# A graph, attention and expert kernel: lists read in 24-byte pieces, later weight requests behind the third gather, another order in the tail

## The chip, the cores and the metric

The kernel runs on one core of a Trainium2 chip. The metric is device time in microseconds for one whole execution; lower is better. The profile comes from one separate, profiled execution.

## The reference, cut to what matters

1250 nodes of 1024 values go through a graph convolution and a linear attention in parallel, and then through a mixture of eight experts, of which each node uses two. The change touches only the experts:

```python
logits = flat @ Wr.T                          # flat: 1250 x 1024, Wr: 8 x 1024
weights, ids = jax.lax.top_k(logits, 2)
weights = softmax(weights)
h = einsum('nc,efc->nef', flat, W1)           # W1: 8 x 512 x 1024
val, gate = h[..., :256], h[..., 256:]
act = val * silu(gate)
expert_outputs = einsum('nef,ecf->nec', act, W2)   # W2: 8 x 1024 x 256
out = einsum('nec,ne->nc', expert_outputs, router_weights)
x = x + out
```

## The kernel before, in words

The layer norm, the graph convolution and the attention take the first four fifths of the time and aren't touched. They leave the residual in `out` and the normalised rows in `flat_d`, both in HBM. The router writes, for every expert, a list of entries (row number, weight; 8 bytes) into `list_d`, by scatters from GpSimd. A list has room for 13 tiles of 128 entries (`LT`), and entries that aren't taken point to filler rows behind row 1249, with weight 0.

The expert stage works on tiles of 128 entries. Each expert has `PER` = 3 tiles, so `TILES` = 24, three after three. Entries beyond 384 of an expert are done as further tiles ("items") in a loop at the end, whose length is read from a register and is at least 1; in the profiled execution it runs once. For a tile n:

- GpSimd gathers its rows from `flat_d` into `xg` (`gather`, six buffers, line 956), steered by `lists[:, n, 0]`.
- XE: TensorE turns the rows into `wide[0]` (line 2214), ScalarE copies them to the high part `xe_h`, VectorE subtracts to get the low part `xe_l`. Every product in this kernel is three products of such parts.
- GV: TensorE multiplies with the four slabs of W1 (line 2236) into `gv`, `kvb` for even and `lsb` for odd tiles, 24 matmuls.
- SM: ScalarE takes the silu of half of it into `sil`, VectorE multiplies it with the other half into `act`.
- TR: TensorE turns `act` (line 2220), ScalarE copies to `a_h`, VectorE subtracts to `a_l`.
- OUT: TensorE multiplies with W2 (line 2228, 12 matmuls), ScalarE scales into `y`, GpSimd scatters with addition into `out` (line 968).
- WP and W2P: each slab of W1 (512 KB, `ws_raw`, four buffers) and each W2 (1 MB, `w_raw`, one buffer) is loaded by SP and split by ScalarE (`ws_h`, `w_h`) and VectorE (`ws_l`, `w_l`). W2P covers one expert.

The order of ScalarE's and VectorE's work is written out in `expert_steps` (line 279); TensorE's is the loop over tiles below line 2240, which puts XE of tile n+1 and TR of tile n-1 inside GV of tile n, and OUT of tile n-1 behind it. The engines wait for each other by counters (`expert_full`, `expert_act`, `expert_dve`), whose values `numbered` works out from the same lists.

SP asks for the first expert's weights early, then, when the router is done, for the eight lists (line 829), one request each, 8-byte pieces, so that tile i of an expert holds entries 128 i to 128 i + 127. Right behind it asks for the next weights (line 705, 709), each as soon as its buffer is split. GpSimd starts the first six gathers as the lists land.

The tail begins behind GV of tile 23. Silu and product of tile 23 aren't in the ordinary steps; they and the further steps of the last tile are the head of the loop over items (`silu_tail`, `act_tail`, `finish`). One turn of that loop finishes the tile before (SM, TR, OUT), turns the item's rows, splits the item's weights, and runs the item's GV; on VectorE it then works out which item comes next (`item_link`, `next_item`, eight small operations on one partition, lines 1724 to 1730). Behind the loop the last item is finished in the same way. The list of the previous tile, which ScalarE's scale and the scatter need, is read again by SP once the scatter before has landed (lines 863, 875).

Of the kernel before, what the change touches and what calls it, by code (L numbers as in the profile page):

```python
# [16 lines left out]
F32 = mybir.dt.float32  # L17
# [6 lines left out]
ALU = mybir.AluOpType  # L24
ACT = mybir.ActivationFunctionType
# [253 lines left out]
def expert_steps():  # L279

    o = [("WP", m) for m in range(SLABS_PER)] + [("W2P", 0), ("XE", 0)]
    for n in range(TILES):
        e, i = divmod(n, PER)
        if e + 1 < EXP:
            o += ([("W2P", e + 1)] if i == PER - 1 else
                  [("WP", SLABS_PER * (e + 1) + 2 * i), ("WP", SLABS_PER * (e + 1) + 2 * i + 1)])
        if n >= 2:
            o.append(("OUT", n - 2))
        if n + 1 < TILES:
            o.append(("XE", n + 1))  # L290
        if n >= 1:
            o.append(("TR", n - 1))
        o.append(("GV", n))
        if n < TILES - 1:
            o.append(("SM", n))
    return o + [("OUT", TILES - 2)]


# [4 lines left out]
for _n in range(TILES):  # L303
    ORDERED_PE += [("XE", _n + 1)] if _n + 1 < TILES else []
    ORDERED_PE += ([("TR", _n - 1)] if _n else []) + [("GV", _n)] + ([("OUT", _n - 1)] if _n else [])
R_FULL = numbered({"XE", "TR", "GV", "OUT"}, [("XE", 0)] + [k for k in ORDERED_PE if k != ("GV", TILES - 1)])
SCATTERED = [len(range(s, TILES - 1, NY)) for s in range(NY)]


def build(nc, x, src_cols, dst_cols, dst_groups, slabs, wv, w1, w2, wr, proj, feat_rows, consts, turns, tie,  # L310
          iota, keys, eye, pe, blank, before, list_blank, tokens, expert_at, item_rows, b2_rows, out):
    ctx = ExitStack()
    with ctx:
# [327 lines left out]
        def _(sp):  # L641
# [183 lines left out]
            sp.wait_ge(routed, 1)  # L825
            sp.wait_ge(lists_free, 1)
            list_tiles = list_d.rearrange("(t q) w -> t q w", q=RT_)
            for e in range(EXP):
                sp.dma_start(lists[:, PER * e:PER * e + PER, :],
                             list_tiles[LT * e:LT * e + PER].rearrange("i q w -> q i w")).then_inc(list_landed[min(e, 2)], 16)  # L830
            for k in STEPS:
                if k[0] == "WP" and k[1] + SLABS_PER < SLABS_PER * EXP:
                    sp.wait_ge(expert_dve, R_DVE[k])
# [166 lines left out]
        def _(act):  # L1000
# [237 lines left out]
                    else:  # L1238
                        ins.then_inc(expert_act, 1)

            def silu_tail(turn, tr_full):

                act.wait_ge(tail_gv, turn)
                act.wait_ge(expert_dve, R_DVE[("SM", TILES - 2)])
                act.activation(sil[:, :], gv[1][:, 0:FF], ACT.Silu).then_inc(tail_act, 1)
                act.wait_ge(tail_full, tr_full)
                copy(a_p[1][0][:, :, :].rearrange("p f c -> p (f c)"), turned[1]).then_inc(tail_act, 1)

# [7 lines left out]
            act.wait_ge(items_ready, 1)  # L1256
            items = act.value_load(items_n[0:1, 0:1], min_val=1, max_val=MAX_ITEMS)
            with act.Fori(0, items) as r:
                silu_tail(r + 1, r * 3 + 2)
                copy(xe_p[0][0][:, :, :], blocks(wide[0], KD, RT_, 128)).then_inc(tail_act, 1)  # L1260
                for m in range(SLABS_PER):
                    if m == 2:
                        out_tail(r * 3 + 3, r * 16 + 16, r * 16 + 16 * SCATTERED[NY - 1])
                    act.wait_ge(ws_landed[m], r * 16 + 16 * (EXP + 1))
                    copy(ws_p[m][0][:, :, :], ws_raw[m][:, :, :]).then_inc(tail_act, 1)
                act.wait_ge(w2_landed, r * 16 + 16 * (EXP + 1))
                copy(w2_p[1][0][:, :, :], w2_raw[:, :, :]).then_inc(tail_act, 1)
            silu_tail(items + 1, items * 3 + 1)
            out_tail(items * 3 + 2, items * 16 + 16, items * 16 + 16 * SCATTERED[NY - 1])


        @block.vector
        def _(dve):
# [472 lines left out]
            for k in STEPS:  # L1746
                kind, n = k
                if kind == "WP":
                    hi, lo = ws_p[n % (2 * SLABS_PER)]
                    acted(k)  # L1750
                    ins = tt(lo[:, :, :], ws_raw[n % SLABS_PER][:, :, :], hi[:, :, :].bitcast(F32), ALU.subtract)
                    if n >= SLABS_PER * (EXP - 1):
                        ins.then_inc(raw_split, 1)
                        dve.wait_ge(raw_split, n - SLABS_PER * (EXP - 1) + 1)
                        dve.sem_inc(expert_dve, 1)
                    else:
                        ins.then_inc(expert_dve, 1)
                elif kind == "W2P":
                    hi, lo = w2_p[n % 2]
                    acted(k)  # L1760
                    ins = tt(lo[:, :, :], w2_raw[:, :, :], hi[:, :, :].bitcast(F32), ALU.subtract)
                    if n == EXP - 1:
                        ins.then_inc(w2_split, 1)
                        dve.wait_ge(w2_split, 1)
                        dve.sem_inc(expert_dve, 1)
                    else:
                        ins.then_inc(expert_dve, 1)
                elif kind == "XE":
                    hi, lo = xe_p[n % 2]
                    acted(k)  # L1770
                    ins = tt(lo[:, :, :], blocks(wide[0], KD, RT_, 128), hi[:, :, :].bitcast(F32), ALU.subtract)
                    if n == TILES - 1:
                        ins.then_inc(tail_xe, 1)
                        dve.wait_ge(tail_xe, 1)
                        dve.sem_inc(expert_dve, 1)
                    else:
                        ins.then_inc(expert_dve, 1)
                elif kind == "SM":
                    acted(k)
                    if n >= 2:  # L1780
                        dve.wait_ge(expert_full, R_FULL[("TR", n - 2)])
                    tt(act_t[n % 2][:, :], gv[n % 2][:, FF:2 * FF], sil[:, :], ALU.mult).then_inc(expert_dve, 1)
                elif kind == "TR":
                    hi, lo = a_p[n % 2]
                    acted(k)
                    tt(lo[:, :, :].rearrange("p f c -> p (f c)"), turned[n % 2],
                       hi[:, :, :].bitcast(F32).rearrange("p f c -> p (f c)"), ALU.subtract).then_inc(expert_dve, 1)

            def act_tail(turn):

                dve.wait_ge(tail_act, turn * 8 + 1)
                tt(act_t[1][:, :], gv[1][:, FF:2 * FF], sil[:, :], ALU.mult).then_inc(tail_low, 1)
                dve.wait_ge(tail_act, turn * 8 + 2)
                tt(a_p[1][1][:, :, :].rearrange("p f c -> p (f c)"), turned[1],
                   a_p[1][0][:, :, :].bitcast(F32).rearrange("p f c -> p (f c)"), ALU.subtract).then_inc(tail_low, 1)

            items = dve.value_load(items_n[0:1, 0:1], min_val=1, max_val=MAX_ITEMS)
            with dve.Fori(0, items) as r:
                act_tail(r)
                dve.wait_ge(tail_act, r * 8 + 3)  # L1800
                tt(xe_p[0][1][:, :, :], blocks(wide[0], KD, RT_, 128), xe_p[0][0][:, :, :].bitcast(F32), ALU.subtract
                   ).then_inc(tail_xe, 1)
                for m in range(SLABS_PER):
                    dve.wait_ge(tail_act, r * 8 + m + 4)
                    tt(ws_p[m][1][:, :, :], ws_raw[m][:, :, :], ws_p[m][0][:, :, :].bitcast(F32), ALU.subtract
                       ).then_inc(raw_split, 1)
                dve.wait_ge(tail_act, r * 8 + 8)
                tt(w2_p[1][1][:, :, :], w2_raw[:, :, :], w2_p[1][0][:, :, :].bitcast(F32), ALU.subtract
                   ).then_inc(w2_split, 1)
                dve.wait_ge(item_read, r + 1)  # L1810
                item_link(ts(item_x[:, 2:3], first, GAP, ALU.add), r)
                next_item(r)
                dve.sem_inc(item_made, 1)
            act_tail(items)


        @block.tensor
        def _(ten):
# [429 lines left out]
            for n in range(TILES):  # L2248
                e = n // PER
                dved(("XE", n))  # L2250
                for kt in range(KD):
                    m = SLABS_PER * e + kt // 2
                    if n % PER == 0 and kt % 2 == 0:
                        dved(("WP", m))
                    mm = gate_value_part(n % 2, xe_p[n % 2], ws_p[m % (2 * SLABS_PER)], kt)
                    if kt == 1 and n + 1 < TILES:
                        expert_rows(n + 1)
                    if kt == 3 and n:
                        dved(("SM", n - 1))
                        act_turned((n - 1) % 2).then_inc(expert_full, 1)  # L2260
                mm.then_inc(expert_full if n < TILES - 1 else tail_gv, 1)
                if n:
                    dved(("TR", n - 1))
                    dved(("W2P", (n - 1) // PER))
                    if n >= 2:
                        ten.wait_ge(expert_act, R_ACT[("OUT", n - 2)])
                    out_product((n - 1) % 2, w2_p[(n - 1) // PER % 2]).then_inc(expert_full, 1)
# [103 lines left out]
```

## Time and profile before

| | |
|---|---|
| median of 3 timed runs | 1466.77 us (1465.06 to 1468.51) |
| the profiled execution's own time | 1471.01 us |
| its span, first to last instruction | 1469.3 us |
| TensorE matmul busy in the span | 1382.0 us (94%) |
| mean granted clock of TensorE | 0.977 |
| VectorE, ScalarE, GpSimd busy | 60%, 36%, 11% |
| DMA queue 1 (requests of SP) | 33.5% of the 16 engines' span |
| DMA queue 0 (requests of GpSimd) | 16.0% |

Busy shares are means over stages with different limits. In the page's 40 slices TensorE is busy nine tenths or more nearly throughout; slice 33, from about 1175 to 1212 us, shows 2 tenths, and the last shows 4.

### The profile page before, as it was taken

Reading aid. Unit: us, or ns where it says so; the run is one execution under the profiler, and the core shown is the slowest. Engines: PE = TensorE matmul, PEld = TensorE weight load, DVE = VectorE, ACT = ScalarE, POOL = GpSimd, SP = SyncE. Lnnn points to the kernel's source line nnn. Section 1 sums busy time; section 2 is a strip of 40 time slices with the busy share of each in tenths; the row PEclk is TensorE's granted clock in tenths of the full one; section 3 lists DMA queues with packets and bytes.
Section 4 is the critical chain, followed back from the end, with each engine's and each line's share of the span. In section 5 each row is a group of like instructions: output and inputs, shape, how many; then the busy total and the mean of one; then the engine's idle time right before and its main releaser. Section 6 shows DMA issues by size and latency. Waiting matters only on the chain.

```text
span 1469.3 us, 19184 instructions
## 1 busy us (share of the span) xinstructions
PE 1382.0 (94%) x7433; PEld 1266.9 (86%) x7433; DVE 875.9 (60%) x1600; ACT 534.3 (36%) x629; POOL 166.7 (11%) x169
## 2 busy tenths in 40 slices
PE   6999999999999999899999999999999929999994
PEld 5788989999999999899999999999878728888883
DVE  6455668788787787636656333355567854444423
ACT  4223245454444544423122133322211235555523
POOL 0011211101101101000000000000000531222211
PEclk9999999999999999999999999999999959999997
DMA  9865422432432434867453033221564577888843
GB/s 299 245 156 125 88 52 32 99 81 31 98 78 35 98 78 101 309 152 195 107 146 104 15 99 110 67 85 35 144 184 140 140 242 219 226 227 230 230 101 57
DMA packets 99181, 193.22 MB, mean 132 GB/s; under 512 B 33905, under 2 KB 64617, under 8 KB 97372
## 3 DMA queue, kind: packets, MB, share of 16 engines
q1 hardware_dynamic: 79171, 145.83, 33.5%
q0 software_dynamic: 19920, 46.17, 16.0%
q8 instruction: 59, 0.97, 0.3%
q14 instruction: 31, 0.25, 0.1%
HBM read 129.38 MB, written 72.21 MB: 137 GB/s over the span
## 4 chain that ended last, share of the span: by engine, by line
PE 74%; DMA 11%; DVE 8%; ACT 4%; issue 2%; POOLq 0%; SPq 0%; ACTq 0%; POOL 0%; DVEq 0%
PE slot L2032 23%; PE slot L2119 13%; DMA adj_d<-stage 6%; PE slot L2189 5%; PE slot L2228 5%; PE kvb L2236 5%; PE lsb L2236 4%; PE slot L1988 3%; PE kvb L2153 3%; PE slot L2001 3%; PE slot L1974 2%; PE slot L1963 2%; PE slot L2214 2%; DMA mix_d<-mixn 1%; PE slot L1943 1%
## 5 line engine op out<-in xcount | busy, mean ns | idle before, releaser
L2032 PE MATMUL slot<-big_hi,slab_h 128*128 128x418 f32 x768 | 194.6, 362 | 10.1 <-DVE qp_l L1558 4.8
L2032 PE MATMUL slot<-big_lo,slab_h 128*128 128x418 f32 x768 | 189.3, 355 | 0.0
L2032 PE MATMUL slot<-big_hi,slab_l 128*128 128x418 f32 x768 | 188.4, 354 | 0.0
L2032 PEld LDWEIGHTS slot<-big_hi,slab_h 128*128 128x128 f32 x768 | 139.7, 190 | 15.0 <-DVE qp_l L1558 6.4
L2032 PEld LDWEIGHTS slot<-big_hi,slab_l 128*128 128x128 f32 x768 | 145.3, 189 | 2.2
L2032 PEld LDWEIGHTS slot<-big_lo,slab_h 128*128 128x128 f32 x768 | 145.3, 189 | 2.0
L908 POOL DMA_DIRECT2D adj_d<-stage x80 | 67.3, 842 | 485.0 <-ACT stage L1012 328.5
L2119 PE MATMUL slot<-adj,xs_h 125*128 125x418 f32 x480 | 118.1, 354 | 0.5 <-DVE ztmp L1283 0.5
L2119 PE MATMUL slot<-adj,xs_l 125*128 125x418 f32 x480 | 117.5, 353 | 0.0
L1287 DVE TENSOR_SCALAR oh_src<-lane,src_lo 125x125 bf16<-125x125 f16 x320 | 83.7, 262 | 30.0 <-PE kvb L1848 21.0
L2119 PEld LDWEIGHTS slot<-adj,xs_h 125*128 125x128 f32 x480 | 90.5, 189 | 1.7 <-DVE ztmp L1283 0.7
L2119 PEld LDWEIGHTS slot<-adj,xs_l 125*128 125x128 f32 x480 | 90.5, 189 | 1.2
L1287 DVE TENSOR_SCALAR oh_key<-key_iota,key_rel 125x240 bf16<-125x240 int16 x320 | 90.2, 282 | 0.0
L933 POOL DMA_INDIRECT list_d<-rec,spots x20 | 28.1, 1404 | 521.8 <-issue 504.5
L1283 DVE TENSOR_TENSOR slab_l<-slab_raw,slab_h 128x1024 fp32r<-128x1024 f32 x34 | 41.6, 1223 | 48.7 <-ACT slab_h L1012 48.5
L1572 DVE RECIPROCAL nrm<-nrm 128x1254 f32<-128x1254 f32 x8 | 63.9, 7993 | 9.6 <-ACT nrm L1012 9.6
L1283 DVE TENSOR_TENSOR xe_l<-slot,xe_h 128x1024 fp32r<-128x1024 f32 x25 | 30.6, 1224 | 62.2 <-ACT xe_h L1012 62.2
L1541 DVE SCALAR_TENSOR_TENSOR kk_l<-slot,kk_h 125x512 fp32r<-125x512 f32 x80 | 52.2, 687 | 23.6 <-ACT kk_h L1146 22.8
L1146 ACT ACTIVATE kk_h<-slot 125x512 fp32r<-125x512 f32 x80 | 47.5, 596 | 44.7 <-PE slot L1963 44.3
L1558 DVE SCALAR_TENSOR_TENSOR qp_l<-slot,qp_h 128x1254 fp32r<-128x1254 f32 x30 | 43.9, 1464 | 29.6 <-ACT qp_h L1158 29.6
L968 POOL DMA_INDIRECT out_dram<-y,lists x23 | 36.3, 1578 | 169.4 <-ACT y L1012 142.3
L2153 PE MATMUL kvb<-kk_h,v_h 125*128 125x256 f32 x160 | 47.1, 295 | 6.7 <-DVE kk_l L1541 6.7
(334 smaller groups left out, 2902.4 us busy)
## 6 DMA issues: line engine op xcount, KB each, us to landing
slab_raw<-slabs_dram SPq DMA_DIRECT2D x40, 512.0 KB, 4.3
ws_raw<-w_dram SPq DMA_DIRECT2D x36, 512.0 KB, 4.8
adj_d<-stage POOLq DMA_DIRECT2D x81, 117.2 KB, 3.1
w_raw<-w_dram SPq DMA_DIRECT2D x9, 1024.0 KB, 5.4
adj_d<-eye_dram POOLq DMA_DIRECT2D x1, 6250.0 KB, 24.0
raw<-adj_d SPq DMA_DIRECT2D x3, 1828.8 KB
dx<-x_dram SPq DMA_DIRECT2D x10, 448.0 KB
xn_d<-dx SPq DMA_DIRECT2D x10, 448.0 KB
```

Of the source, the lines that this page charges most:

```text
L908: pool.dma_start(adj_d[:, bass.ds(first, SPAN), :].rearrange("p d j -> p (d j)"), stage[g % 3][:, :], accum_op=ALU.add).then_inc(e_added, 16)
L1146: act.activation(kk_p[k[2] % 3][0][:, :], kk_bank(k), ACT.Relu).then_inc(act_done, 1)
L1283: return dve.tensor_tensor(o, a, b, op)
L1287: dve.tensor_scalar(o, a, s1, None, op0)
L1541: dve.scalar_tensor_tensor(out=kk_p[k[2] % 3][1][:, :], in0=kk_bank(k), scalar=0.0, in1=kk_p[k[2] % 3][0][:, :].bitcast(F32), op0=ALU.max, ...
L1572: link(dve.reciprocal(nrm[:, :], nrm[:, :]))
L2032: mm = ten.matmul(ps[:, 512 * q:512 * q + CW], w[a][:, kt, :], big[b][:, kt, CW * q:CW * q + CW], start=(kt == 0 and c == 0), stop=(kt == ...
L2119: mm = ten.matmul(ps[:, 512 * q:512 * q + CW], xs_p[t % 2][a][:, j, :], adj[:, j, CW * q:CW * q + CW], start=(j == 0 and a == 0), stop=(j ...
L2153: mm = ten.matmul(kvb[:, FEAT * h:FEAT * h + FEAT], v_p[a][:, i, 64 * h:64 * h + 128], kk_p[i % 3][b][:, FEAT * h:FEAT * h + FEAT], start= ...
L2189: mm = ten.matmul(ps[:T, 512 * q:512 * q + 512], big[b][:, kt, T * i:T * i + T], rows_p[kt][a][:, 512 * q:512 * q + 512], start=(kt == 0 a ...
L2228: mm = ten.matmul(wide[1][:RT_, 512 * q:512 * q + 512], a_p[s_][a][:, f, :], w_[b][:, f, 512 * q:512 * q + 512], start=(f == 0 and c == 0) ...
L2236: mm = ten.matmul(gv[s_][:RT_, :], xe[a][:, kt, :], w_[b][:, kt % 2, :], start=(kt == 0 and c == 0), stop=(kt == KD - 1 and c == 2))
```

## The change

It does three things.

1. SP reads the lists of the first seven experts with partition q taking the three neighbouring entries 3q to 3q+2 of the list, one piece of 24 bytes, so tile i of these experts holds the entries 3q + i. The last expert's list is read tile by tile as before.
2. Between the lists and the later weight requests SP waits until the gathers 0, 1 and 2 have landed.
3. The silu and product of tile 23 go into the ordinary steps. The item loop begins with the transposed copy (`high_tail`, `low_tail`) and ends with silu and product of the item; VectorE works out the next item at the head of the loop; ScalarE makes three slab copies ahead of the previous tile's output instead of two.

```diff
@@ expert_steps
-        o.append(("GV", n))
-        if n < TILES - 1:
-            o.append(("SM", n))
+        o += [("GV", n), ("SM", n)]
@@ SP
-            for e in range(EXP):
-                sp.dma_start(lists[:, PER * e:PER * e + PER, :],
-                             list_tiles[LT * e:LT * e + PER].rearrange("i q w -> q i w")).then_inc(list_landed[min(e, 2)], 16)
+            for e in range(EXP - 1):
+                sp.dma_start(lists[:, PER * e:PER * e + PER, :].rearrange("q i w -> q (i w)"),
+                             list_d[LIST * e:LIST * e + CAP, :].rearrange("(q i) w -> q (i w)", i=PER)
+                             ).then_inc(list_landed[min(e, 2)], 16)
+            sp.dma_start(lists[:, TILES - PER:TILES, :], list_tiles[LT * (EXP - 1):LT * (EXP - 1) + PER].rearrange("i q w -> q i w")
+                         ).then_inc(list_landed[2], 16)
+            for n in range(3):
+                sp.wait_ge(gathered[n], 16)
             for k in STEPS:
@@ ScalarE
-            def silu_tail(turn, tr_full):
-
-                act.wait_ge(tail_gv, turn)
-                act.wait_ge(expert_dve, R_DVE[("SM", TILES - 2)])
-                act.activation(sil[:, :], gv[1][:, 0:FF], ACT.Silu).then_inc(tail_act, 1)
+            def high_tail(tr_full):
+
                 act.wait_ge(tail_full, tr_full)
                 copy(a_p[1][0][:, :, :].rearrange("p f c -> p (f c)"), turned[1]).then_inc(tail_act, 1)
@@
             with act.Fori(0, items) as r:
-                silu_tail(r + 1, r * 3 + 2)
+                high_tail(r * 3 + 2)
                 copy(xe_p[0][0][:, :, :], blocks(wide[0], KD, RT_, 128)).then_inc(tail_act, 1)
                 for m in range(SLABS_PER):
-                    if m == 2:
+                    if m == 3:
                         out_tail(r * 3 + 3, r * 16 + 16, r * 16 + 16 * SCATTERED[NY - 1])
@@
                 copy(w2_p[1][0][:, :, :], w2_raw[:, :, :]).then_inc(tail_act, 1)
-            silu_tail(items + 1, items * 3 + 1)
+                act.wait_ge(tail_gv, r + 1)
+                act.activation(sil[:, :], gv[1][:, 0:FF], ACT.Silu).then_inc(tail_act, 1)
+            high_tail(items * 3 + 1)
@@ VectorE
-            def act_tail(turn):
+            def low_tail(turn):
 
                 dve.wait_ge(tail_act, turn * 8 + 1)
-                tt(act_t[1][:, :], gv[1][:, FF:2 * FF], sil[:, :], ALU.mult).then_inc(tail_low, 1)
-                dve.wait_ge(tail_act, turn * 8 + 2)
                 tt(a_p[1][1][:, :, :].rearrange("p f c -> p (f c)"), turned[1],
@@
             with dve.Fori(0, items) as r:
-                act_tail(r)
+                dve.wait_ge(item_read, r + 1)
+                item_link(ts(item_x[:, 2:3], first, GAP, ALU.add), r)
+                next_item(r)
+                dve.sem_inc(item_made, 1)
+                low_tail(r)
...
                 tt(w2_p[1][1][:, :, :], w2_raw[:, :, :], w2_p[1][0][:, :, :].bitcast(F32), ALU.subtract
                    ).then_inc(w2_split, 1)
-                dve.wait_ge(item_read, r + 1)
-                item_link(ts(item_x[:, 2:3], first, GAP, ALU.add), r)
-                next_item(r)
-                dve.sem_inc(item_made, 1)
-            act_tail(items)
+                dve.wait_ge(tail_act, r * 8 + 8)
+                tt(act_t[1][:, :], gv[1][:, FF:2 * FF], sil[:, :], ALU.mult).then_inc(tail_low, 1)
+            low_tail(items)
```

## Rows read from the trace of the kernel before

**Rows 1.** Busy time by stretch: us, each engine (instructions), clock, DMA share, GB/s

```profile
1260.00:1430.00 170.00, 170.00 (x837) 141.63 (x836) 71.14 (x80) 79.77 (x97) 44.29 (x35) 1.00 0.78 205
```

**Rows 2.** The chain that ended last, 1190 to 1220: start us, us, what

```profile
1197.49 8.44 DMA xg<-flat_d,lists
1206.07 1.96 PE slot L2214 x8
...
1219.11 1.36 PE lsb L2236 x6
```

**Rows 3.** Order of time, 1190 to 1216: start, us, engine, line, out<-in, count [idle before]

```profile
1194.58 4.12 SPq L829 DMA_DIRECT2D lists<-list_d  x8
1196.45 2.29 DVE L1283 TENSOR_TENSOR w_l<-w_raw,w_h 128x2048 fp32r<-128x2048 f32 x1
1197.49 2.12 POOL L956 DMA_INDIRECT xg<-flat_d,lists  x1 [5.64 <-DMA lists<-list_d]
1198.74 2.00 SPq L705 DMA_DIRECT2D ws_raw<-w_dram  x4
1199.91 0.96 POOL L956 DMA_INDIRECT xg<-flat_d,lists  x1 [0.30 <-issue]
...
1215.04 1.03 ACT L1012 ACTIVATE xe_h<-slot 128x1024 fp32r<-128x1024 f32 x1 [4.08 <-PE slot L2214]
```

**Rows 4.** DMA view: packets 1202 to 1203; time to landing of the gather of 1453.79

```profile
q1 hardware_dynamic: 58, 0.22, 53.0%
q0 software_dynamic: 42, 0.17, 50.2%
...
xg<-flat_d,lists POOLq DMA_INDIRECT x1, 3.9
```

**Rows 5.** Order of time, VectorE and GpSimd about 1162, GpSimd at 1454

```profile
1161.61 1.22 DVE L1615 SCALAR_TENSOR_TENSOR acc<-acc,xm 125x1024 f32<-125x1024 f32 x1
1161.69 2.21 POOL L933 DMA_INDIRECT list_d<-rec,spots  x1 [0.30 <-issue]
...
1453.79 1.00 POOL L990 DMA_INDIRECT xg<-flat_d,lists  x1 [8.90 <-DMA lists<-list_d]
```

**Rows 6.** DMA view, landing: second slab of 1199.3, gathers 1194.5 to 1215, scatter 1443.3

```profile
ws_raw<-w_dram SPq DMA_DIRECT2D x1, 512.0 KB, 7.0
...
xg<-flat_d,lists POOLq DMA_INDIRECT x6, 11.0
...
out_dram<-y,lists POOLq DMA_INDIRECT x1, 6.0
```

**Rows 7.** The chain that ended last, 1429 to 1458

```profile
1429.58 2.74 PE slot L2228 x12
...
1434.36 0.39 ACT sil L1245
...
1435.73 0.39 ACT a_h L1012
...
1436.62 4.63 PE slot L2228 x12
...
1452.85 5.03 PE slot L2228 x12
```

**Rows 8.** Busy time by stretch, the output product of tile 23

```profile
1436.60:1440.20 3.60, 3.58 (x9) 2.81 (x10) 3.14 (x3) 2.31 (x3) 0.00 (x0) 0.53 0.74 127
```

**Rows 9.** Order of time, ScalarE and VectorE from 1436.9 to 1451

```profile
1436.91 2.00 ACT L1012 ACTIVATE ws_h<-ws_raw 128x1024 fp32r<-128x1024 f32 x2
...
1441.42 1.12 ACT L1012 ACTIVATE y<-slot,lists 128x1024 f32<-128x1024 f32 x1 [2.51 <-PE slot L2228]
...
1444.33 1.91 ACT L1012 ACTIVATE w_h<-w_raw 128x2048 fp32r<-128x2048 f32 x1
...
1446.27 2.29 DVE L1283 TENSOR_TENSOR w_l<-w_raw,w_h 128x2048 fp32r<-128x2048 f32 x1 [0.39 <-ACT w_h L1012]
...
1448.48 0.13 DVE L1287 TENSOR_SCALAR item_x<-item_w 1x1 int32<-1x1 f32 x1
...
1450.57 0.42 DVE L1283 TENSOR_TENSOR act<-lsb,sil 128x256 f32<-128x256 f32 x1 [0.41 <-DVE item_w L1730]
```

More of the change, by code:

```diff
@@ L305 @@
     ORDERED_PE += ([("TR", _n - 1)] if _n else []) + [("GV", _n)] + ([("OUT", _n - 1)] if _n else [])
-R_FULL = numbered({"XE", "TR", "GV", "OUT"}, [("XE", 0)] + [k for k in ORDERED_PE if k != ("GV", TILES - 1)])
+R_FULL = numbered({"XE", "TR", "GV", "OUT"}, [("XE", 0)] + ORDERED_PE)
 SCATTERED = [len(range(s, TILES - 1, NY)) for s in range(NY)]
@@ L1781, in _ @@
                         dve.wait_ge(expert_full, R_FULL[("TR", n - 2)])
-                    tt(act_t[n % 2][:, :], gv[n % 2][:, FF:2 * FF], sil[:, :], ALU.mult).then_inc(expert_dve, 1)
+                    tt(act_t[n % 2][:, :], gv[n % 2][:, FF:2 * FF], sil[:, :], ALU.mult
+                       ).then_inc(expert_dve if n < TILES - 1 else tail_low, 1)
                 elif kind == "TR":
@@ L1798, in _ @@
             with dve.Fori(0, items) as r:
-                act_tail(r)
[L1800 to L1809, printed above, removed]
                 dve.wait_ge(item_read, r + 1)
@@ L1813, in _ @@
                 dve.sem_inc(item_made, 1)
-            act_tail(items)
+                low_tail(r)
+                dve.wait_ge(tail_act, r * 8 + 2)
+                tt(xe_p[0][1][:, :, :], blocks(wide[0], KD, RT_, 128), xe_p[0][0][:, :, :].bitcast(F32), ALU.subtract
+                   ).then_inc(tail_xe, 1)
+                for m in range(SLABS_PER):
+                    dve.wait_ge(tail_act, r * 8 + m + 3)
+                    tt(ws_p[m][1][:, :, :], ws_raw[m][:, :, :], ws_p[m][0][:, :, :].bitcast(F32), ALU.subtract
+                       ).then_inc(raw_split, 1)
+                dve.wait_ge(tail_act, r * 8 + 7)
+                tt(w2_p[1][1][:, :, :], w2_raw[:, :, :], w2_p[1][0][:, :, :].bitcast(F32), ALU.subtract
+                   ).then_inc(w2_split, 1)
+                dve.wait_ge(tail_act, r * 8 + 8)
+                tt(act_t[1][:, :], gv[1][:, FF:2 * FF], sil[:, :], ALU.mult).then_inc(tail_low, 1)
+            low_tail(items)
         @block.tensor
@@ L2260, in _ @@
                         act_turned((n - 1) % 2).then_inc(expert_full, 1)
-                mm.then_inc(expert_full if n < TILES - 1 else tail_gv, 1)
+                mm.then_inc(expert_full, 1)
                 if n:
```

## The prediction

> **What bounds the kernel now.** I read the busy times by stretch first, then the chain of work that ended last, then the order of time and the DMA views around the two places the change touches. The stretch table shows that from 1260 to 1430 us TensorE is busy 170.00 of 170 us at the full clock while the 16 DMA engines are 0.78 busy [rows 1]. Nothing in the change takes work from TensorE there, so the middle of the expert stage can't move. What can move is the stall ahead of it and the tail behind it. In the chain the stall reads: the first gather is issued at 1197.49 and lands 8.44 us later, TensorE turns its rows at 1206.07 (1.96 us), and after their split it has product after product; tile 1's begins at 1219.11 [rows 2]. In the tail TensorE, ScalarE and VectorE take turns on the chain.
>
> **Start: what the moved weight requests are worth.** Before, SP asks for slabs 4 to 7 and the second W2 from 1198.74 on, right behind the lists, and so before the first gather has moved a byte [rows 3]. In the microsecond from 1202 both kinds run together: 58 packets of q1 (weights), 42 of q0 (gather), each at about half of the engines' time [rows 4]. The gather of the same 128 rows that runs with no other large traffic, the one issued at 1453.79, lands in 3.9 us [rows 4]. Its issuing instruction takes 1.00 us against 2.12 for the first gather [rows 3, 5], so I add 1.1 and get 5.0: landing at 1197.49 + 5.0 = 1202.5 in place of 1205.9. **Gain 3.4 us**, if everything behind it follows; the low clock of TensorE's first products moves along, since it starts from the same idle state. Both ends: 0 if the weights aren't what delays it; 8.44 - 3.9 = 4.5 at most, if the long issue goes too.
>
> **Start: what the 24-byte lists are worth.** Seven lists of 128 pieces replace seven of 384. SP spends 4.12 us on eight requests [rows 3]; that may fall by a microsecond, and the first list may land some 0.2 to 0.3 us sooner. I cost this at nothing, because the first gather's instruction seems to be held by something else. VectorE is in w_l, with two SBUF inputs, from 1196.45 to 1198.74; 2.12 us after 1197.49 is 1199.61, and that is 1198.74 plus 0.87, about the 0.96 that the next gather takes [rows 3]. The same picture stands at 1161.69: a scatter that starts inside a VectorE operation (until 1162.83) takes 2.21 us and ends 1.07 behind it [rows 5]. So a gather that starts 0.3 us sooner still ends its issue at 1199.6. The Trainium skill says the same of the mechanism (SBUF — State Buffer, "SBUF: two separate sides"): VectorE and GpSimd share a port pair as an exclusive lock, held for a whole instruction. By that rule the sooner list is worth 0; without it the gather would land at 1197.2 + 3.9 = 1201.1, 1.4 us sooner still. The other six lists were never waited for. The interleaved order puts as many rows of 4 KB into each gather and scatter as before, some of them filler rows in each tile rather than nearly all in the third: cost 0, with the cover that the DMA engines have 22% free.
>
> **Start: what the added wait costs.** Behind SP's wait for gather 2 stand the weights of expert 1. GpSimd starts a gather every 1.25 us, so gather 2 lands about 1201.2 + 3.9 = 1205.1, up to 1206. The second slab request landed 7.0 us after its issue while sharing with gathers [rows 6]. Hence slab 4 lands by about 1210 and slab 5 between 1211.2 (the bytes of all gathers and two slabs at the 400 GB/s seen there) and 1205.7 + 7.0 = 1212.7. ScalarE takes slabs 4 and 5 in order *ahead* of the second tile's rows (xe_h), where it stood idle 4.08 us before [rows 3]. With everything 3.4 us earlier, tile 1's product can start at 1219.11 - 3.4 = 1215.7 [rows 2]; slab 5 at 1212.7 gives split 1213.7, xe_h 1214.8, xe_l by 1216.2: a stall of 0.5 us at worst, none at 1211.2. Slabs 6 and 7 and W2 are split one and two tiles later and have some microseconds. I take 0.
>
> **Tail, first half.** Today the last tile's silu waits until the item loop has begun: sil at 1434.36, product with the gate, transposes, a_h at 1435.73 [rows 7]. After the change silu and product of tile 23 run in the ordinary order at 1429.6, while TensorE still does the 2.74 us output product of tile 22, and the transposes follow the row transposes at 1433.2. ScalarE's loop entry stays, so a_h comes at 1434.36: **1.37 us** sooner, and tile 23's output product starts at 1435.25 and not 1436.62. It took 4.63 us on the chain, 4.46 to the next product's first matmul, because the clock had fallen (granted 0.53 of full, so 1.2 GHz for nearly all of it [rows 8]) after TensorE had done next to nothing since 1433.2. Now it has stood only 1.8 us, so I expect full clock and 2.74: 1.7 us more. ScalarE then goes three ws_h (1.0 us each, from 1435.54), y (1.12), ws_h, w_h (1.91): done at 1442.5; VectorE's w_l (2.29) ends at 1444.8 against 1448.56 today [rows 9]: **3.8 us** sooner. If the clock falls all the same, y comes at 1439.8 and this is 2.5.
>
> **Tail, second half.** Today eight small VectorE operations on the item list stand between w_l and the last product with the gate: from 1448.48 to 1450.57 [rows 9]. They move to the loop's start, where VectorE has only to be done by a_h at 1434.75; they take 1.7 us from about 1431, so they are covered by ScalarE's y and loop entry (uncovered they would cost up to 1.7). That takes **2.0 us** more off, so the last act starts at 1444.8 and not 1450.57, 5.8 us sooner. From act to the last output product today takes 2.28 us at low clock, and from sil's act to tile 23's product 1.85 [rows 7, 9]; I take 1.85: start at 1446.65. The product itself takes 5.0 at low clock today; I take 4.55, as the clock still falls in this gap half the time. It ends at 1451.2. The last y also needs the last list, which SP asks for once tile 23's scatter has landed: issue about 1440.5 (0.8 behind y, which ends at 1439.7), 6.0 us as today [rows 6] to 7.8 with the gather now right behind it, list 1.8 more: between 1448.3 and 1450.1, just in time. So y starts at 1451.3 in place of 1458.06: **6.8 us** for the tail. Ends: 4.5 (clock low twice) and 7.9 (clock full twice, then the list is late).
>
> **Sum.** The profiled execution took 1471.01 us, with a span of 1469.3; 3.4 + 6.8 = 10.2 leaves 1460.8 and 1459.1. The median of the timed runs is 1466.77, 4.2 below the profiled one, and the stages are the same, so I subtract from it: **1456.6 us**.
>
> **Rivals.** (1) The first gather doesn't land sooner: its 8.44 us would then be list packets and first use, not weights. Against it stands that q0 got half of each microsecond from 1202; for it, that the list packets of 8 bytes share the engines just before. Only the tail is gained: 1466.8 - 6.8 = 1460.0. (2) Clock low in tile 23's output product: 1.3 us less, 1457.9. (3) Late weights: slab 5 later than 1212.2 costs one for one. If gather 2 took 11.0, the median of today's first six [rows 6],, slab 5 would land at 1219.7 and stall 7 us: 1463.9. (4) Slower than before: DMA becomes the bound. If rows scattered over the whole node range, and filler rows in every tile, made gathers and scatters dearer, the 0.78 share [rows 1] would reach 1 at 28% more; from there each per cent costs 0.0726 us in each of 22 tiles, 1.6 us. It decides from 34% on, where the 10 us are used up; at 40% the time is 1456.6 + 19 = 1476. Nothing in the trace speaks for it: both orders read rows of 4 KB. (5) The change doesn't do what it says the other way: the issue isn't held by VectorE, and the sooner list counts: 1.4 us more, 1455.2.
>
> **Numbers.** Forecast 0.60 (own range 1454 to 1459), gather unmoved 0.13, clock low 0.12, late weights 0.07, DMA bound 0.02, sooner list 0.06. The range 1453 to 1461.5 covers all but most of the late weights and the DMA bound, and leaves 1.5 us for how medians of one kernel differ (1465.06 to 1468.51 before). About 0.2%, 2.9 us, is what a measurement can tell, so faster means under 1463.8: 0.93; within 0.04; slower 0.03.
>
> **What would show it.** The first gather's time to landing: near 5 us. TensorE's first transposes about 8.1 us behind the first list request's issue, where they are 11.5 behind it now. No idle TensorE ahead of tile 1's product. The issue of the first gather still about 2.1 us long. In the tail the last act's idle time ended by w_l or silu, not by item_w; tile 23's output product at full clock. The forecast is wrong if the first gather still takes over 7 us, if TensorE stands before tile 1's product, or if the last list lands behind the last output product by microseconds.

## The result, and the profile after

The median is 1459.48 us of six runs (1457.73 to 1462.0), beside 1468.99 of six of the kernel before: ratio 0.9941, interval [0.9925, 0.9957]. The profiled execution took 1460.71 us with a span of 1459.0, against 1471.01 and 1469.3, so 10.3 us less where the prediction's sum had 10.2. Both halves have the predicted sign, and both were mis-sized: y of tile 22 starts at 1430.06 and not 1432.34, so all ahead of it gave 2.28 us and not 3.4 (0.33 of it, 1194.58 to 1194.25, was there at SP's first list request, where nothing had changed yet); from there to the last y it is 17.64 us and not 25.72, so the tail gave 8.08 and not 6.8. That the two errors nearly cancel in this profile is luck; how much the tail's share of it varies is shown below.

The chain of work that ended last, changed kernel (start us, us, what), at the start of the expert stage:

```profile
1194.25 2.23 DMA lists<-list_d
...
1197.43 4.82 DMA xg<-flat_d,lists
...
1202.38 1.96 PE slot L2217 x8
...
1206.52 6.51 DMA ws_raw<-w_dram
...
1213.05 1.07 ACT ws_h L1015
...
1216.56 1.65 PE lsb L2239 x6
```

The gather takes 4.82 where [rows 2] has 8.44. But in [rows 2] the chain goes from the gather through the turning and the split of tile 0's rows, and from there on TensorE alone to tile 1's product; now it leaves TensorE behind that split and passes through a weight slab that SP asked for at 1206.52. That is a new wait, and the order of time shows what it costs (start, us, engine, line, out<-in, count [idle before]):

```profile
1197.43 1.47 POOL L959 DMA_INDIRECT xg<-flat_d,lists  x1 [6.29 <-DMA lists<-list_d]
1206.14 1.83 SPq L703 DMA_DIRECT2D ws_raw<-w_dram  x4
1211.76 1.06 ACT L1015 ACTIVATE ws_h<-ws_raw 128x1024 fp32r<-128x1024 f32 x1 [6.37 <-DMA ws_raw<-w_dram]
1213.05 1.06 ACT L1015 ACTIVATE ws_h<-ws_raw 128x1024 fp32r<-128x1024 f32 x1 [0.23 <-DMA ws_raw<-w_dram]
1216.56 0.50 PE L2239 MATMUL lsb<-ws_h,xe_h 128*128 128x512 f32 x1 [1.50 <-DVE xe_l L1285]
```

ScalarE waits for slab 4, then for slab 5, and tile 1's xe_h stands behind them; TensorE idles 1.50 us. Counted from the first list request, tile 1's product begins at 22.31 where it was 24.36. (The chain of [rows 2] writes 1219.11 for it, the end of the matmul before; its own first matmul started at 1218.94, in the order of time:)

```profile
1218.94 0.39 PE L2236 MATMUL lsb<-ws_h,xe_h 128*128 128x512 f32 x1
```

The DMA view says why the slabs are late; packets and MB of queues 0 (gathers) and 1 (weights), from 1208 to 1209 and from 1209 to 1210:

```profile
q0 software_dynamic: 86, 0.32, 80.9%
q1 hardware_dynamic: 7, 0.03, 9.1%
...
q1 hardware_dynamic: 67, 0.27, 72.6%
q0 software_dynamic: 28, 0.07, 17.5%
```

The weights were asked for at 1206.14, and 2.9 us later they had moved 7 packets: gathers 3 to 5 were in the queues first. Not all of the 2.9 is owed to them. In the trace the first weight packet comes 2.3 us behind the request; in the kernel before, with no packet of a gather ahead of it, it came 1.1 behind (at 1199.86, for the request at 1198.74).

The middle of the stage, busy time by stretch as in [rows 1]: TensorE is as full as before, with the DMA engines at 0.80. (The 0.78 of [rows 1] is over ten microseconds more; from 1260 to 1420 the kernel before has 0.79.) From the transposes of tile 2 to y of tile 22 both kernels take 212.0 us.

```profile
1260.00:1420.00 160.00, 160.00 (x791) 133.37 (x791) 69.43 (x77) 77.89 (x94) 41.40 (x32) 1.00 0.80 209
```

The tail. First both output products by stretch (clock is the third number from the end), then the chain:

```profile
1432.93:1435.80 2.87, 2.87 (x13) 2.19 (x13) 2.43 (x3) 2.87 (x4) 0.65 (x1) 1.00 0.63 66
1444.28:1447.20 2.92, 2.92 (x12) 2.14 (x12) 0.00 (x0) 0.00 (x0) 0.00 (x0) 1.00 0.64 208
```

```profile
1430.06 1.12 ACT y L1015
...
1432.02 6.21 DMA out_dram<-y,lists
...
1439.28 6.35 DMA out_dram<-y,lists
...
1445.85 1.74 DMA lists<-list_d
...
1447.70 1.12 ACT y L1015
```

The two products took 4.63 and 5.03 in [rows 7]; the first of them had a clock of 0.53 in its first 3.6 us [rows 8], and the second, from 1452.85 to its end, one of 0.57. Now both run at full clock (2.4 GHz), and neither is on the chain: it runs over scatter 22, for which GpSimd waits, scatter 23, the last list, and the last y, for which ScalarE idles 4.12 us until the list is there. The last output product ends at 1447.26, the list lands 0.3 us later and y begins at 1447.70, so TensorE and the DMA chain are nearly level.

### The profile page after: what moved, and what is told of

Read it like the earlier page. It is cut to its first block, busy times and chain, and to the rows that moved or that the text cites. A ratio compares the mean times of both kernels' runs of the same rounds, so it can differ in the third digit from the quotient of the medians.

```text
span 1459.0 us, 19184 instructions
## 1 busy us (share of the span) xinstructions
PE 1377.8 (94%) x7433; PEld 1264.4 (87%) x7433; DVE 876.8 (60%) x1600; ACT 534.7 (37%) x629; POOL 167.1 (11%) x169
## 4 chain that ended last, share of the span: by engine, by line
PE 74%; DMA 12%; DVE 7%; ACT 3%; issue 2%; POOLq 0%; SPq 0%; POOL 0%; ACTq 0%; DVEq 0%
PE slot L2035 24%; PE slot L2122 13%; DMA adj_d<-stage 6%; PE slot L2192 5%; PE lsb L2239 5%; PE slot L2231 4%; PE kvb L2239 4%; PE slot L1991 3%; PE slot L2004 3%; PE kvb L2156 3%; PE slot L1977 2%; PE slot L1966 2%; PE slot L2217 1%; DMA mix_d<-mixn 1%; PE slot L1946 1%
## 5 line engine op out<-in xcount | busy, mean ns | idle before, releaser
L1289 DVE TENSOR_SCALAR oh_src<-lane,src_lo 125x125 bf16<-125x125 f16 x320 | 84.0, 263 | 29.1 <-PE kvb L1851 20.4
L1161 ACT ACTIVATE qp_h<-slot 128x1254 fp32r<-128x1254 f32 x30 | 36.6, 1219 | 45.8 <-PE slot L1977 45.1
```

The costliest lines, as they stand in the source:

```text
L1289: dve.tensor_scalar(o, a, s1, None, op0)
```

## The experiments

Three times are compared below: from SP's first list request to the row transposes of tile 2 ("start", 25.73 before, 23.80 after), from there to y of tile 22 (212.0 wherever TensorE's clock is full by then), and from there to the last y ("tail", 25.72 and 17.64). What lies ahead of the first list request varies between executions by more than most effects here (that request is issued between 1187.65 and 1198.56); a single time says little, the stage times much more. They vary too: the changed kernel's start, run in four profiles with nothing altered in it (after, items_late, busy_tail, after_again), took 23.80, 24.41, 24.63 and 24.25, and the start before 25.73 and 25.79 (tail_only). Most experiments below have one profile, so a start between 23.8 and 24.6 is no news.

Five kernels were timed once each: rows_first 1466.21, w2_behind_rows 1466.24, items_late 1463.44 and busy_tail 1456.97, beside one execution of the kernel before of 1467.52, and busy_start 1457.59 beside one of 1463.90. Nothing is concluded from these times.

**The wait alone.** The kernel before with

```diff
+            for n in range(3):
+                sp.wait_ge(gathered[n], 16)
             for k in STEPS:
```

> The kernel before with only the added wait of SP for gathers 0, 1 and 2. Theory (weights delay the first gather): the first gather, still issued about 2.1 us long, lands 5 us after its issue instead of 8.4; slab 5 comes about 1.5 us too late for tile 1, as in the changed kernel; tile 1's product starts 2.0 us sooner than before, so the time is about 0.15% less. Rival (list packets or first use delay it): the first gather still takes over 7 us, and the late weights make the time longer by about 1.5 us.

Ratio 1.0 [0.9982, 1.0018]. In its profile the rows of tile 0 are turned 5.66 us behind the gather's issue (8.58 before), tile 1's product waits 1.75 us for the late slabs and begins 1.5 sooner (22.85 behind the first list request, not 24.36), where 2.0 had been expected; the start is 24.37. That is 1.4 gained, too little for the times to show, and within what the changed kernel's start takes with the new lists.

**The lists alone.** The kernel before with the diff's two new list requests.

> The kernel before with only the seven lists in pieces of 24 bytes. Theory: SP's eight list requests take 3.6 us instead of 4.1, the weights are asked for half a microsecond sooner, the first gather's issue still ends 0.9 us behind VectorE's w_l, and it lands no sooner than before (8.0 to 9.0 us); the DMA share from 1260 to 1430 stays 0.78; time within 0.1% of before. Rival (list packets were in the gather's way): it lands in 5 to 6 us and 2 us come off. Rival (scattered rows are dearer): the DMA share goes up by 0.05 or more.

Ratio 0.9998 [0.9977, 1.0019]. SP is done with the lists 0.5 us sooner (weights asked for 3.69 behind the first list request, not 4.16). The rows of tile 0 are turned 9.36 behind the gather's issue, and the start is 26.73, 1.0 worse in this one profile. Some 0.4 of that is not owed to the lists: w_l, and with it the issue, ended later behind the first list request (5.45, not 5.03). The other 0.5 lies behind the issue's end (6.96 for 6.46), and goes with weights that are asked for sooner. The chain that ended last, lists alone:

```profile
1197.33 9.22 DMA xg<-flat_d,lists
...
1206.69 1.95 PE slot L2217 x8
```

Its order of time shows VectorE's hold again: the gather starts inside w_l, takes 2.40, and ends 0.9 behind it, after the first weight request:

```profile
1196.56 2.28 DVE L1286 TENSOR_TENSOR w_l<-w_raw,w_h 128x2048 fp32r<-128x2048 f32 x1
1197.33 2.40 POOL L959 DMA_INDIRECT xg<-flat_d,lists  x1 [5.36 <-DMA lists<-list_d]
1197.97 1.91 SPq L705 DMA_DIRECT2D ws_raw<-w_dram  x4
```

The DMA share is 0.80 from 1260 to 1420, against 0.79 before, and TensorE is busy throughout: the interleaved order costs nothing there.

**The tail alone.** The kernel before with the third part of the diff.

> The kernel before with only the change of the tail (silu of tile 23 in the ordinary steps, next item at the head of the loop, three slab copies ahead of y). Theory: from the end of tile 22's output product to the last y 17.6 us instead of 25.7, 8 us less, nothing changed ahead of it: ratio about 0.9945. Rival (the tail's gain hangs on the moved start through the clock's phase): 5 to 6.5 us less, with TensorE at half clock in one of the two last output products.

1460.8 us, ratio 0.9957 [0.9941, 0.9974]: most of what the whole change brings. Its tail is 18.84, 6.9 less than before, between the 8 of the theory and the 5 to 6.5 of the rival: the clock fell in tile 23's product (0.66 from 1432 to 1437) and was full in the last.

**Waiting for one gather and not three.** The changed kernel with

```diff
-            for n in range(3):
-                sp.wait_ge(gathered[n], 16)
+            sp.wait_ge(gathered[0], 16)
```

> The changed kernel, but SP waits for gather 0 alone before it asks for slabs 4 to 7. Theory (the wait for the third gather costs a stall of 1.5 us of TensorE ahead of tile 1's product): requests at 1202.3, slab 5 landed by about 1210, no idle TensorE before tile 1, gather 0 still about 4.8 us; 1.5 us less than the changed kernel. Rival (slabs are late because gathers hold the engines whatever the request's time): slab 5 lands no sooner than 1212 and the stall stays. Rival: gather 1 becomes late and tile 0's product stops for it.

1457.71 us, 0.9924 [0.99, 0.9948], overlapping the changed kernel's interval. The weights are asked for 3.3 us sooner, but ScalarE still waits for both slabs:

```profile
1211.22 1.06 ACT L1014 ACTIVATE ws_h<-ws_raw 128x1024 fp32r<-128x1024 f32 x1 [4.14 <-DMA ws_raw<-w_dram]
1213.78 1.06 ACT L1014 ACTIVATE ws_h<-ws_raw 128x1024 fp32r<-128x1024 f32 x1 [1.50 <-DMA ws_raw<-w_dram]
```

The stall ahead of tile 1's product falls from 1.50 to 0.43, the start to 23.44, 0.4 below the lowest of the four. Slab 5 came far later than expected: for two microseconds from the request at 1203.96 all packets are gathers'. When the weights are asked for matters less than what is queued ahead of them.

**Rows ahead of slabs.** The changed kernel with XE of tile 1 ahead of slabs 4 and 5 on ScalarE and VectorE.

```diff
     for n in range(TILES):
+        if n == 0:
+            o.append(("XE", 1))
...
-        if n + 1 < TILES:
+        if n and n + 1 < TILES:
```

> The changed kernel, with tile 1's rows (xe) ahead of slabs 4 and 5 in the written order of ScalarE and VectorE. Theory (ScalarE waits for the late slabs 4 and 5 while tile 1's rows lie ready): the slabs land as late as in the changed kernel, 6.9 us or more after the rows' request order begins, but TensorE doesn't stop ahead of tile 1's product (idle under 0.2 us in place of 1.5), and from the first list request to tile 2's row transposes 22.3 us instead of 23.8. Rival (slabs late for their own use): the stop only moves, to slab 8's product or to tile 2, and no time comes off.

TensorE has no idle time ahead of tile 1's product, but the start is 23.65 and not the 22.3 expected. Part of it is the gather: tile 0's rows came at 8.72 behind the first list request (8.13 in the changed kernel, 8.13 to 9.15 in the four profiles). From there to tile 2's row transposes it is 14.93 us, against 15.48 to 15.79 in the four, so taking the stall away is worth 0.6 to 0.9. The rest went to the clock: tile 0's product was at half clock until 10.0 us behind the turning of its rows, 8.3 in the changed kernel.

**The issue freed, with no wait.** The kernel before with one swap in ScalarE's and VectorE's order, so that the split of the first W2 (w_h on ScalarE, w_l on VectorE) comes behind tile 0's rows:

```diff
-    o = [("WP", m) for m in range(SLABS_PER)] + [("W2P", 0), ("XE", 0)]
+    o = [("WP", m) for m in range(SLABS_PER)] + [("XE", 0), ("W2P", 0)]
```

> The kernel before, with the split of the first W2 (w_h, w_l) moved behind the rows of tile 0 on ScalarE and VectorE, so that VectorE is idle when the first gather is issued. Theory (the issue is held by w_l): the first gather's issuing instruction takes 0.9 to 1.2 us instead of 2.1. Rival (a first gather is slow by itself): 2.1 us as before. It still shares the engines with the weights, so it lands 7.5 us or more after its issue.

```profile
1195.50 1.00 POOL L956 DMA_INDIRECT xg<-flat_d,lists  x1 [6.80 <-DMA lists<-list_d]
1196.22 2.15 SPq L705 DMA_DIRECT2D ws_raw<-w_dram  x4
...
1195.50 5.57 DMA xg<-flat_d,lists
...
1214.30 1.36 PE lsb L2236 x6
```

(order of time, then the chain that ended last). The issue takes 1.00 and not 2.12, as expected. The gather then lands in 5.57 though the weights are asked for as early as before, where I had expected 7.5 or more. There is no stall, and the start is 23.43: 2.3 us gained, no less than the changed kernel gains, and SP waits for nothing. So weights asked for early don't by themselves make the gather as late as it was. The runs without SP's wait line up by the order of the two: the end of the first gather's issue is measured against SP's first weight request; then, behind the issue's end, the gather's first packet of 4 KB in the trace, and the turning of the rows.

| kernel | issue ends behind the weight request | first packet behind the issue's end | rows turned behind the issue's end |
|---|---|---|---|
| best (below) | 0.18 | 0.75 | 4.69 |
| w2_behind_rows | 0.28 | 0.72 | 4.70 |
| hold_free (below) | 0.54 | 2.01 | 4.84 |
| before | 0.87 | 2.10 | 6.46 |
| tail_only | 1.02 | 2.88 | 6.60 |
| lists_only | 1.76 | 3.32 | 6.96 |
| eight with the wait | (weights much later) | 0.69 to 0.72 | 3.45 to 3.84 |

With nothing ahead of it the gather's first packet comes 0.7 behind the issue's end, and the first weight packet 1.1 behind its request (1.11 to 1.13 in hold_free, before, tail_only and lists_only). In best and w2_behind_rows the gather's packets are first, and the weights' first comes 2.7 and 2.5 behind the request; in the other four the weights are first and the gather starts late. That order doesn't explain everything. In hold_free the weights were first too, and the rows were in time all the same; and with the gather first it still takes 0.8 to 1.3 us more than with the weights held back. How late a gather lands once it has begun stays open.

**The item's operations back at the end.** The changed kernel with VectorE's item steps again between w_l and the last act.

> The changed kernel, but the eight small VectorE operations on the item list stand again between w_l and the last product with the gate. Theory: the last act starts 2.0 us behind w_l's end instead of at once, all else equal; TensorE then idles 3.3 us ahead of the last output product and is at half clock in it, so from the end of tile 22's output product to the last y 21 to 23 us, against 17.6 in the changed kernel's profile. Rival (the last list or the scatter sets the end): last y within 1 us of the changed kernel's, as they start at the same time.

The tail is 20.80, 3.2 more. TensorE stands 3.10 us ahead of the last transposes (1.19 in the changed kernel), so 1.9 is the operations themselves; the rest is the clock, 0.64 in the last product, which takes 4.48 and not 2.98. Expected were 21 to 23, so the effect is there at a little under the lower end; and as the low clock came in four of the seven tails below too, only the 1.9 is surely owed to the operations.

**TensorE kept busy in the tail.** The changed kernel with 5, 4 and 3 products that nobody reads, in the waits around the two output products:

```diff
                 act_turned(1).then_inc(tail_full, 1)
+                keep_busy(5 if turn is not items else 3, 0)
...
                 mm.then_inc(tail_gv, 1)
+            keep_busy(4, 0)
```

> The changed kernel with 5, 4 and 3 products that nobody reads, put on TensorE where it waits in the tail: ahead of tile 23's output product, ahead of the last transposes, ahead of the last output product. Theory (the tail's length hangs on whether the clock falls in these waits: 17.6 us without a fall, 18.8 with one, 20.4 with two): clock 1.00 from 1431 to the last output product, 17.4 to 17.9 us from tile 22's output product to the last y. Rival (the clock falls by its own time): a granted clock of 0.5 in one of the two output products all the same.

The clock stays full and the tail is 17.57, level with the changed kernel's profile: there the clock had held by itself. That is not the rule. Of seven tails with this order and no extra products, the last output product ran at full clock in three and at 0.62 to 0.64 in four (wait_for_one, rows_first, busy_start, hold_free), and tile 23's product was slow in two (wait_for_one, tail_only). With no fall the tail is 17.6 to 17.9, with one 18.8 to 19.0, with two 20.4. TensorE's idle times ahead of the products are the same in all seven (1.8, then 1.2 to 1.3 and 1.1 us), so nothing that I can see in the trace decides it. With the extra products both were at full clock in two tails of two (busy_tail and best), without them in two of seven (after, after_again): that points their way, but two profiles don't prove it.

**TensorE kept busy at the start.** The changed kernel with 18 such products between the first weights' split and the first rows, and 6 between the rows and tile 0's product:

```diff
+            dved(("WP", 3))
+            early(18)
             expert_rows(0)
+            early(6)
```

> The changed kernel with 18 more products of 128 x 512 between the split of the first expert's weights and the first rows, and 6 between the turning of those rows and the first tile's product; nobody reads what they write. They stand in time in which TensorE waits for the lists and the first gather. If the low clock of the first tile's product is owed to TensorE having stood idle before it, the granted clock is full from the first tile on, and with it tile 0's product takes some 1.5 to 2 us less; but then the stall before tile 1's product (1.50 in the changed kernel) grows by as much, since the late slabs set when tile 1 can start: from the first list request to tile 2's row transposes still 23.0 to 23.8 us. If instead TensorE's own work sets that time, it falls by 1.5 to 2 us to about 22. The rival that the clock doesn't depend on it gives the same clock as in the changed kernel. Tail as in the changed kernel, 17.6, or 18.8 if the clock falls once.

```profile
1196.28 1.08 PE L2217 MATMUL slot<-ident,xg 128*128 128x128 f32 x8
1197.12 1.64 PE L2253 MATMUL lsb<-ws_h 128*128 128x512 f32 x6
1199.73 0.50 PE L2239 MATMUL kvb<-ws_h,xe_h 128*128 128x512 f32 x1 [0.97 <-DVE xe_l L1285]
...
1210.37 0.50 PE L2239 MATMUL lsb<-ws_h,xe_h 128*128 128x512 f32 x1 [3.98 <-DVE xe_l L1285]
```

The rows are turned in 1.08 and not 1.94 us, and tile 0's product at full clock ends before 1206.4; the stall grows from 1.50 to 3.98 and the start is 24.35, no better. The clock falls again in the longer stall (0.50 from 1212 to 1214), and this costs beyond the start: from there to y of tile 22 it is 213.5 us in place of 212.0. With the wait in SP, the late slabs set when tile 1 begins, and what TensorE saves ahead of them is lost, here with 1.5 us more.

**Without the wait, and the best of it.** On the same chip: the changed kernel again; "hold_free", the changed kernel without SP's wait and with the swap of the W2 split; "best", which is hold_free with the unread products at the start and in the tail.

> The changed kernel once more, for a direct comparison with the two kernels that follow: 1459.5 us, 8 below the kernel before.

> The changed kernel without SP's wait for gathers 0 to 2, and with the split of the first W2 behind the split of tile 0's rows. If the gather came late because VectorE held its issue until the weights were ahead of it in the queues, freeing the issue does what the wait does: the first gather's issue takes 1.0, its rows are turned 5.7 behind it, no stall ahead of tile 1's product, from the first list request to tile 2's transposes 23.4 (changed kernel 23.8), the median within 1 us of the changed kernel. If the wait is what keeps the weights out of the gather's way (asked for 3.7 behind the first list request with the new lists, and not 4.2), the first gather takes 8 or more again and the time is 2 to 3 us above the changed kernel.

> hold_free with the products that nobody reads, both at the start (18 and 6) and in the tail (5, 4, 3). With the weights asked for early nothing late stands behind tile 0's product, so here the full clock should count, where with the wait it didn't: tile 0's rows turned in 1.1 and not 1.9, its product 6.5 and not 8.1; tile 1's product 19.1 to 20 behind the first list request, no stall, tile 2's transposes at 20.7 to 21.5, against 23.8 in the changed kernel. The tail stays 17.6. Median 2 to 3.5 us below the changed kernel: 1456 to 1457.5. If the slabs, which then share the engines with six gathers, come later than tile 0's product ends, most of it turns into a stall and the median is that of the changed kernel.

| kernel | median us | ratio to before | start | tail |
|---|---|---|---|---|
| after_again | 1460.97 | 0.9946 [0.9927, 0.9965] | 24.25 | 17.90 |
| hold_free | 1459.72 | 0.9939 [0.9907, 0.9970] | 24.02 | 18.82 |
| best | 1454.88 | 0.9908 [0.9887, 0.9928] | 19.83 | 17.52 |

hold_free takes away the wait with no loss that shows (the intervals overlap): the issue takes 1.00, the rows are turned 5.84 behind it, no stall. In best, from the split of the first rows on, the chain is TensorE alone:

```profile
1198.95 1.24 DVE xe_l L1283
1200.23 1.65 PE kvb L2237 x6
1201.89 0.87 PE slot L2215 x8
1202.76 4.13 PE kvb L2237 x18
1206.89 1.36 PE lsb L2237 x6
```

The start is 19.83, somewhat under the 20.7 to 21.5 expected; with the same unread products that gave nothing with the wait it is 4.2 us shorter than hold_free's, 0.5 of it because tile 0's rows came sooner (8.56 behind the first list request, not 9.07). The median is 6.1 us below the changed kernel of the same comparison, more than the 2 to 3.5 expected. The stage times explain 4.4 + 0.4 of it (24.25 to 19.83, 17.90 to 17.52); what makes up the remaining 1.3 isn't shown; the changed kernel's five times alone lie 7.9 us apart. The two intervals just touch, at 0.9927.

## Why the prediction was right, point by point

The time, 1456.6, and the range 1453 to 1461.5 held the median of 1459.48; the kernel is faster, by 0.59%. Of the 2.9 us between forecast and median, 2.2 are the base: the kernel before had 1466.77 in the three runs known then and 1468.99 in the six beside the result. The single terms did less well than their sum, and that the sum came out is partly luck: the start gave 2.28, with the 0.33 that was there before it, where 3.4 was said; the tail made up for it with 8.08 for 6.8, because its clock stayed full, as in two tails of the seven that have this order.

- **The gather of 5.0 us** came as 4.82, closer than the reasoning earned. The issue took 1.47 and not 2.1, and what lies behind it took longer than in the lone gather. In six more profiles with the wait (all but after_again) the issue took 1.9 to 2.4, and the rows were turned 5.52 to 5.90 behind its start, not 4.95. The cause was told half right. I had the gather sharing the engines with weights. They do share from 1202 on [rows 4], and with the weights held back the rows come 0.8 to 1.4 us sooner behind the issue's end than in the kernels with a freed issue and early weights. But the larger part, 1.8 of the time behind the issue's end, is gone once the issue, held by w_l, is freed (w2_behind_rows, 5.57 in all against the same early weights). So the prediction's bound, "4.5 at most, if the long issue goes too", treated as a small extra what is by itself enough.
- **The sooner list worth nothing** was right, and for the reason given. In all eleven profiles with w_l in its old place the issue ends 0.86 to 0.89 behind it whenever it starts (it is 2.12 long in before, 2.40 in lists_only, 1.47 in the changed kernel), and in the three with w_l moved it takes 1.00. The Trainium skill's exclusive lock (SBUF — State Buffer, "SBUF: two separate sides") agrees with these fourteen. The first list wasn't sooner anyway (2.23 us to landing). That the last six lists cost nothing may have hidden a loss: done sooner, SP asks for the weights sooner, which goes with 0.5 us in the one profile of lists_only. In the changed kernel the wait covers this.
- **The added wait costed at 0, at worst 0.5** was the step that failed. TensorE stands 1.50 us for it (1.01 to 1.50 in the four profiles with this start), of which rows_first shows 0.6 to 0.9 to be time that can be won back. I let slab 4 land by 1210 and slab 5 between 1211.2 and 1212.7, and took the early end. They came for ScalarE at 1211.76 and 1213.05 (the two ws_h rows above), in the prediction's times 0.33 later still. The term that was too small is gather 2, which landed 5.6 and not 3.9 us behind its issue: the gather "with no other large traffic" of [rows 4] has no other gathers beside it either. So SP's wait ended at 1206.14, and slab 5 was asked for at 1206.52 and not 1205.7. The 7.0 of [rows 6] was not too small: slab 5 took 6.51. The early end was never near, as gathers alone moved 0.32 to 0.37 MB per us and not the 0.40 of that bound. Slab 5 was thus 0.7 later than my late end, and TensorE ready 0.3 sooner than I had it; with the 0.5 that makes the 1.50. The Trainium skill (DMA: Bandwidth & Descriptors, "Queues, rings and completion order") has each engine take turns between the queues that it has work for, packet by packet. That agrees once both run (57 and 49 packets in the microsecond from 1203.49, before). It says nothing of when a request's packets are there to take turns: the weights had 7 of 93 packets from 1.9 to 2.9 us behind their request, where without gathers ahead their first packet came at 1.1.
- **DMA as the bound** was rightly held unlikely: 0.80 for 0.79 over the same stretch, and 212.0 us in both.
- **Tail, first half.** Moved by the 2.28 of the start, a_h came at 1434.32 (predicted 1434.36), w_l's end at 1444.61 (1444.8), act at 1444.53 (1444.8), the last product at 1446.56 (1446.65). The order of work could be read off the trace to 0.3 us.
- **Tail, second half.** I gave the last product 4.55, low clock half of the time; in this profile it took 2.98. Less the 0.3 us for which y then waited for the list, that is the 1.3 us by which the tail exceeded 6.8, and the upper end 7.9 had "clock full twice, then the list is late", which is what happened (8.08, the list 0.3 behind the product's end). Over all runs half was a fair value: low in four of seven.

What the times don't show: the changed kernel and tail_only overlap (0.9941 and 0.9946, beside 0.9957), so that the start's parts bring anything rests on the stage times, 1.1 to 2.0 us (four profiles against two), and not on medians.

## What to carry to other kernels

When a transfer is late, look at the order in which the packets of the queues begin, and at what holds the issuing instruction; moving one split (one operation on ScalarE and one on VectorE) did for the start what a wait with a stall behind it did. A wait that holds requests back must be costed with the queue that it will meet when it ends. And filling TensorE's idle time to keep its clock paid only where nothing late stood behind it: the same products cost 1.5 us behind an unchanged start in one kernel and went with a start shorter by 4.2 us in the other.

## What was not expected of the hardware

- Two DMA queues share about evenly once both move (57 and 49 packets in a microsecond, before), but the one whose first packets come second starts late. A gather's first packet came 0.7 us behind its issue's end with nothing ahead, and 2.0 to 3.3 behind it with weight packets ahead; a weight request's came 1.1 behind it with none of a gather's ahead, and 2.1 to 3.0 with gathers ahead.
- An indirect DMA that GpSimd issued during a VectorE operation with two SBUF inputs ended its issue 0.86 to 0.89 us behind that operation in eleven profiles of eleven, and took 1.00 in the three in which VectorE was free.
- Gathers of 512 KB alone move 0.32 to 0.37 MB per us in all, against 0.40 to 0.41 for weights alone; the third of six lands 5.6 us behind its issue, and one by itself 3.9.
- TensorE's clock fell or held in the tail with the same work and idle times within 0.15 us, from one kernel to the next.
